# Units from 10 on become TensorE's moving rows against regrouped halves of older units, with 33 rounds added before their sum

## The reference

```python
e = jnp.stack([tbl_0[ids[:, 0]], ..., tbl_39[ids[:, 39]]], axis=1)   # 512 x 40 x 64
i_idx, j_idx = np.triu_indices(40, k=1)
viW = jnp.einsum('bpd,pde->bpe', e[:, i_idx, :], L0_rec_W)           # 780 matrices of 64 x 64
z = jnp.einsum('bpe,bpe->bp', viW, e[:, j_idx, :])
h = jnp.concatenate([z, dense_ctx], axis=1)                          # 512 x 796
h = jnp.maximum(h @ W_top1 + b_top1, 0.0)                            # 512 wide
h = jnp.maximum(h @ W_top2 + b_top2, 0.0)                            # 256 wide
y = h @ W_top3
```

## Time and profile before

| | us |
|---|---|
| median of 3 runs | 315.83 (315.57 to 318.13) |
| profiled execution, its own time | 316.28 |
| span of its trace, first to last instruction | 314.0 |
| PE busy | 307.4 (98%) |
| DVE busy | 255.2 (81%) |
| POOL busy | 193.2 (62%) |
| ACT busy | 135.6 (43%) |

### The profile page before, as it was taken

How to read it: one execution, slowest core, us unless ns; L and a number is a source line. 1 busy time by engine, 2 the same in 40 slices (tenths; PEclk the granted TensorE clock), 3 DMA queues, 4 the chain that set the end, 5 groups by cost and what they waited for, 6 DMA issues and landing times.

```text
span 314.0 us, 4400 instructions
## 1 busy us (share of the span) xinstructions
PE 307.4 (98%) x1676; PEld 112.0 (36%) x1676; DVE 255.2 (81%) x262; ACT 135.6 (43%) x338; POOL 193.2 (62%) x156
## 2 busy tenths in 40 slices
PE   7999999999999999999999999999999999999996
PEld 2444233333333323333333333333333333333464
DVE  4992999889898888989989999999999999950000
ACT  0497874875539545659974602066000000001032
POOL 3887777777777777777733887746665555650000
PEclk9999999999999999999999999999999999999999
DMA  5936232323223743232325689886779664440000
GB/s 147 316 113 206 66 92 62 93 61 79 74 62 94 277 149 91 58 92 64 92 54 118 142 192 179 166 191 153 167 167 188 139 135 92 94 83 8 10 0 0
DMA packets 16188, 35.87 MB, mean 114 GB/s; under 512 B 3748, under 2 KB 4776, under 8 KB 14504
## 3 DMA queue, kind: packets, MB, share of 16 engines
q0 software_dynamic: 5824, 16.79, 27.6%
q1 hardware_dynamic: 8264, 14.20, 15.1%
q10 hardware_dynamic: 2080, 4.61, 4.2%
HBM read 22.87 MB, written 0.00 MB: 73 GB/s over the span
## 4 chain that ended last, share of the span: by engine, by line
PE 63%; POOL 24%; issue 8%; DMA 3%; DVE 0%; ACT 0%; ACTq 0%
PE y_ps L671 39%; POOL gathered L338 24%; PE z_ps L695 14%; PE y_ps L705 5%; PE t_ps L705 2%; DMA gathered<-in_tbl,ids_sb 2%; PE y_ps L759 2%; DMA ids_sb<-ids_rows 1%; PE t_ps L759 1%; DVE prod L559 0%; PE y_ps L768 0%; ACT prod L472 0%; ACTq L368 0%; ACT y_out L475 0%; DVE x_fold L527 0%
## 5 line engine op out<-in xcount | busy, mean ns | idle before, releaser
L671 PE MATMUL y_ps<-x,w 64*128 64x512 f32 x780 | 182.8, 604 | 0.9 <-DVE prod L559 0.8
L338 POOL DMA_INDIRECT gathered<-in_tbl,ids_sb x128 | 127.6, 997 | 43.4 <-issue 38.4
L559 DVE TENSOR_TENSOR prod<-y_ps,x 128x1024 f32<-128x1024 f32 x89 | 103.8, 1210 | 15.3 <-PE y_ps L671 14.4
L559 DVE TENSOR_TENSOR prod<-y_ps,x_quad 128x1024 f32<-128x1024 f32 x96 | 110.4, 1214 | 1.3 <-issue 0.6
L671 PEld LDWEIGHTS y_ps<-x,w 64*128 64x128 f32 x780 | 70.2, 186 | 113.4 <-issue 81.3
L410 ACT COPY x<-x_fold 32x128 f32<-32x128 f32 x240 | 70.9, 295 | 68.4 <-DVE x_fold L527 65.7
L363 POOL TENSOR_TENSOR prod<-prod 128x2048 f32<-128x2048 f32 x12 | 54.5, 4540 | 33.2 <-DVE prod L559 33.2
L695 PE MATMUL z_ps<-prod,select 128*32 128x512 f32 x588 | 73.4, 600 | 0.0
L439 ACT COPY zT<-z_ps 128x512 f32<-128x512 f32 x6 | 3.5, 586 | 69.7 <-PE z_ps L695 69.7
L695 PEld LDWEIGHTS z_ps<-prod,select 128*32 128x32 f32 x588 | 14.3, 108 | 52.0 <-issue 36.8
L433 ACT COPY x_mix<-x 64x512 f32<-64x512 f32 x40 | 24.7, 617 | 0.7
(11 more groups left out here) (46 smaller groups left out, 89.1 us busy)
## 6 DMA issues: line engine op xcount, KB each, us to landing
w<-w_rows SPq DMA_DIRECT2D x48, 256.0 KB, 2.8
prod<-prod POOLq DMA_DIRECT2D x12, 1024.0 KB, 7.7
gathered<-in_tbl,ids_sb POOLq DMA_INDIRECT x128, 2.5
w<-w_rows ACTq DMA_DIRECT2D x1, 1792.0 KB, 8.2
prod<-in_tbl ACTq DMA_DIRECT2D x6, 256.0 KB, 7.8
prod<-hot_ids SPq DMA_DIRECT2D x4, 256.0 KB, 6.7
prod<-in_tbl ACTq DMA_DIRECT2D x4, 128.0 KB, 3.0
w<-w_rows ACTq DMA_DIRECT2D x1, 512.0 KB, 9.8
```

Of the source, the lines that this page charges most:

```text
L338: nc.gpsimd.indirect_dma_start(gathered[:, slot, c, s * DIM:(s + 1) * DIM], None, tables[f][:, :], bass.IndirectOffsetOnAxis(ap=ids_sb[:, ...
L559: nc.vector.tensor_tensor(prod[:, d % PROD_SLOTS, :, :], y_ps[:, d % DUO_SLOTS, :, :], factor, ALU.mult).then_inc(prod_ready, 1)
L671: last = nc.tensor.matmul(y_ps[:, d % DUO_SLOTS, half, :], w[rows, r % W_SLOTS, d % ROUND, :], x[rows, units[half], :], start=True, stop=True)
```

## The change

- The pair rounds end with unit 9 (`PAIRED = 10`) instead of 13. From unit 10 on a new unit u supplies the moving rows of PE's matmuls, and the columns are the regrouped halves of all older units c, two units each (`quads_of`). So every unit from 0 to 17 needs its `x_quad` copies: 72 instead of 24, each at the place that `QUAD_AT` names.
- Quad rounds begin at round 11. Of the 37 rounds from 11 to 47, 33 are added: 18 by 1 MB DMAs (12 before) and 15 by POOL (12 before). Round 12 and the rounds 14, 16 and 30 are summed in full. The lag of three begins at round 12 instead of 25; rounds 12 and 13 have no sum, and only round 13 has a block of the first layer in its place.
- 65 gathers are issued first (120 before). The other 63 come in batches of 7, 3 or 4 behind the DMA adds of rounds 11 to 39.
- `x` has 12 slots, `gathered` 4 (6 before), `w` 6 (8 before). Unit u and unit u + 12 share a slot.
- Unit 11 is transposed by PE (before round 12's third duo) instead of folded. `w1` is loaded in seven DMAs behind rounds 3 to 9 instead of one behind round 12. Two one-hots go from ACT to DVE, and two duos are put ahead of the last part of unit 3's pick.

```diff
-LAYER1_AT = [25, 26]
-GATHER_SLOTS = 6
-W_SLOTS = 8
-
-PAIRED = 14
-QUADS = (UNITS - PAIRED) // 2
+NO_SUMS_AT = [12, 13]
+GATHER_SLOTS = 4
+X_SLOTS = 12
+DUOS_AHEAD = 2
+W1_LOADED_AT = 3
+W_SLOTS = 6
+
+PAIRED = 10
+QUADS = UNITS // 2 - 1
...
-           14: (66, 70), 15: (74, 78), 16: (82, 86), 17: (90, 94), 18: (100, 104), 19: (116, 132)}
...
+FOLD_AT = {5: (4, 7), 6: (8, 12), 7: (16, 19), 8: (22, 26), 9: (29, 33), 10: (36, 40), 12: (53, 57), 13: (63, 68),
+           14: (72, 77), 15: (86, 100), 16: (109, 118), 17: (127, 133), 18: (141, 151), 19: (161, 169)}
...
-GATHERED_FIRST = 120
-GATHERS_BEHIND = {24: 2, 26: 2, 28: 2, 30: 2}
...
+GATHERED_FIRST = 65
+GATHERS_BEHIND = {11: 7, 13: 7, 15: 7, 17: 3, 19: 3, 21: 3, 23: 3, 25: 3, 27: 3, 29: 7, 31: 3, 33: 3, 35: 3, 37: 4, 39: 4}
+ADDED_BY_DMA = [11, 13, 15, 17, 19, 21, 23, 25, 27, 29, 31, 33, 35, 37, 39, 41, 43, 45]
+ADDED_BY_POOL = [18, 20, 22, 24, 26, 28, 32, 34, 36, 38, 40, 42, 44, 46, 47]
...
+        self.rounds = [pairs[i:i + ROUND] for i in range(0, len(pairs), ROUND)]
+        self.quads_of([10, 11])
+        self.rounds.append(later + self.mixed(11)[1:])
+        self.quads_of([12, 13])
+        self.quads_of([14, 15])
+        self.rounds.append(self.mixed(11)[:1] + self.mixed(15))
+        self.quads_of([16, 17])
+        self.quads_of([18, 19])
+        self.rounds.append(self.mixed(19))
...
+    def quads_of(self, units):
+
+        items = [(u, c) for u in units for c in range(u // 2)]
+        for (u, c), (v, e) in zip(items[::2], items[1::2]):
+            self.rounds.append([("low", u, c), ("low", v, e), ("high", u, c), ("high", v, e)])
...
             def save_half(u, s):
+                if s == 0 and u >= X_SLOTS:
+
+                    act.wait_ge(prod_ready, plan.last_row(u - X_SLOTS) + 1)
                 act.wait_ge(unit_folded, 2 * list(FOLD_AT).index(u) + s + 1)
...
+            def copy_quad(u):
+                act.wait_ge(x_ready, u + 1)
+                for s in range(2):
+                    for h in range(2):
+                        n = 2 * (u % 2) + s
+                        last = nc.scalar.copy(x_quad[n * QUAD:(n + 1) * QUAD, u - u % 2 + h, :],
+                                              x[s * DIM + h * QUAD:s * DIM + (h + 1) * QUAD, u % X_SLOTS, :])
+                last.then_inc(quad_ready, 1)
...
-                if r == 12:
-                    act.dma_start(w1[:, :, :], w1_in).then_inc(w1_loaded, 16)
...
+                if W1_LOADED_AT <= r < W1_LOADED_AT + NBLK:
+                    b = r - W1_LOADED_AT
+                    act.dma_start(w1[:, b, :], w1_in[:, b, :]).then_inc(w1_loaded, 16)
...
-                if r in LAYER1_AT:
-
-                    n = LAYER1_AT.index(r)
-                    pe.wait_ge(w1_loaded, 32)
-                    pe.wait_ge(z_saved, n + 1)
-                    layer1(0, full[n:n + 1], first=n == 0)
+                if r == NO_SUMS_AT[-1]:
+
+                    pe.wait_ge(w1_loaded, 16 * (NBLK + 1))
+                    pe.wait_ge(z_saved, 1)
+                    pe.wait_ge(x_ready, max(PE_TRANSPOSES_AT) + 1)
+                    layer1(0, full[:1], first=True)
```

More of the change, by code:

```diff
@@ L80, in __init__ @@
         for u in range(PAIRED):
-            pairs += [("pair", k, u) for k in range(u - u % 2)]
+            own = [("pair", k, u) for k in range(u - u % 2)]
+            later = own[-2:] if u == PAIRED - 1 else []
+            pairs += own[:len(own) - len(later)]
             if u % 4 == 3:
                 pairs += self.mixed(u)
[L84 to L99, removed]
+        self.rounds = [pairs[i:i + ROUND] for i in range(0, len(pairs), ROUND)]
[7 more added lines that the diff above has]
+        self.rounds.append(self.mixed(19))
         assert all(len(r) == ROUND for r in self.rounds[:-1])
@@ L109, in __init__ @@
         assert all(self.is_quad(r) for r in ADDED_BY_DMA + ADDED_BY_POOL)
+        assert list(QUAD_AT) == list(range(2 * QUADS))
+    def quads_of(self, units):
+        items = [(u, c) for u in units for c in range(u // 2)]
+        for (u, c), (v, e) in zip(items[::2], items[1::2]):
+            self.rounds.append([("low", u, c), ("low", v, e), ("high", u, c), ("high", v, e)])
     def mixed(self, u):
@@ L118, in sums_at, with last_row @@
     def sums_at(self, r):
-        if r < LAYER1_AT[0]:
+        if r < NO_SUMS_AT[0]:
             return r - EARLY_LAG if r >= EARLY_LAG else None
-        return None if r in LAYER1_AT else r - LAG
+        return None if r in NO_SUMS_AT else r - LAG
     def is_quad(self, r):
         return self.rounds[r][0][0] == "low"
-    def first_round(self, u):
-        if u >= PAIRED:
-            return self.quad_start[(u - PAIRED) // 2]
-        return next(d for d, duo in enumerate(self.duos) if u in duo[1:]) // ROUND
+    def last_row(self, u):
+        return max(d for d, (kind, k, c) in enumerate(self.duos)
+                   if u == k or kind == "pair" and u == c or kind.startswith("mix") and k <= u < k + 4)
     def transposed_at(self, u):
@@ L139, in transposed_at @@
             return FOLD_AT[u][0]
-        return next(d for d, duo in enumerate(self.duos) if u in duo[1:])
+        return PE_TRANSPOSES_AT[u]
     def tile_pairs(self, d, half):
@@ L413, in save_half, with mix_columns, begin_mixture @@
                     last.then_inc(x_ready, 1)
-                if s == 1 and u >= PAIRED:
-                    act.wait_ge(x_ready, u + 1)
-                    for s in range(2):
-                        for h in range(2):
-                            n = 2 * (u % 2) + s
-                            last = nc.scalar.copy(x_quad[n * QUAD:(n + 1) * QUAD, u - PAIRED - u % 2 + h, :],
-                                                  x[s * DIM + h * QUAD:s * DIM + (h + 1) * QUAD, u, :])
-                    last.then_inc(quad_ready, 1)
-            def save_mixture(k):
+            def copy_quad(u):
[6 more added lines that the diff above has]
+                last.then_inc(quad_ready, 1)
+            def mix_columns(k, units):
+                for n, kind in enumerate(("mix1", "mix2")):
+                    for half, (_, columns) in enumerate(plan.mixture(kind, k)):
+                        for side, (unit, field) in enumerate(columns):
+                            if unit in units:
+                                copied = nc.scalar.copy(x_mix[side * DIM:(side + 1) * DIM, 2 * n + half, :],
+                                                        x[field * DIM:(field + 1) * DIM, unit % X_SLOTS, :])
+                return copied
+            def begin_mixture(k):
                 if k:
@@ L625, in pick_unit @@
                 if u == HOT_UNITS - 1:
+                    for d in range(DUOS_AHEAD):
+                        interact(d)
                     transpose_unit(HOT_UNITS)
@@ L671, in interact @@
                     last = nc.tensor.matmul(y_ps[:, d % DUO_SLOTS, half, :], w[rows, r % W_SLOTS, d % ROUND, :],
-                                            x[rows, units[half], :], start=True, stop=True)
+                                            x[rows, units[half] % X_SLOTS, :], start=True, stop=True)
                 last.then_inc(y_ready, 1)
```

72 lines of the change are left out of this document (43 added, 29 removed).

## The result

| | before | after |
|---|---|---|
| median, us | 315.70 (4 runs, 315.51 to 318.13) | 353.64 (4 runs, 352.52 to 354.75) |
| profiled execution, us | 316.28 | 352.52 |
| span of its trace, us | 314.0 | 350.3 |
| PE busy, us | 307.4 (98%) | 317.1 (91%) |

The ratio is 1.1153, with a 95% interval of 1.1093 to 1.1214. The forecast was 350.7, in a range from 324 to 365.

What follows compares the result with a forecast made beforehand. PE bounds the kernel, and DVE as much in added rounds. The 37 rounds take 218.6 us instead of 185.9, +32.7; with 1.3 for block 0 and 0.9 at the end, +34.9: 350.7, range 324 to 365.

Steps and rivals of the forecast that it cites:

- As much the bound as PE: In added rounds DVE's products take 4.57 us and PE 4.62, so DVE bounds there as much as PE.
- The row on which all rests: Gathers queued behind a 1 MB add wait: first 8.2 us after its start, second 9.0, third 9.8, fourth 10.6.
- The rival that went by it: Gathers do not wait for the DMA add ahead of them: 310.3 us; chance 0.10.
- waits of 40.4: DVE's waits for gathers behind DMA adds, at the folds of units 12 to 19: 40.4 us, 20 with lower bounds.
- at full clock: The forecast's own case: waits behind adds while PE's clock stays full, 350.7 us; chance 0.78.
- 40.4 + 0.9 + 2.3: Rounds 11 to 47: gather waits 40.4 us, DVE's loss in round 12 0.9, the wait for block 4's save 2.3.
- The rival that the clock falls: PE's clock halves at its pauses, 4.7 us for each of 12, giving 407 us; chance 0.05.
- `z_saved`: PE waits for block saves standing behind copies in ACT's queue: 1.3 us for block 0, 2.3 for block 4.
- as gone: The wait for the late gather at 111.36, put down to the single 1.75 MB `w1` load: 1.9 us removed.
- The end: One block of the first layer moves from a round to the end: 0.9 us more.
- What would show it: Signs: some 12 DVE gather waits, 40 us in all; PE's share about 86%; 516 sum instructions, some 64 us.
- Half-clock slices: A sign that the forecast is wrong, which would put the time far above the range.

Runs made afterwards that it cites:

- the run with both causes removed: Changed kernel with the half-folds of units 12 to 19 up to 4 duos later and `MIX_AT` of unit 16 at 180 instead of 169: 316.76 us, ratio 1.0006.
- the run with zeros: Changed kernel with 4 to 18 matmuls of zeros for PE at nine folds, fitted to the length of each pause: 353.87 us, ratio 1.1172.
- The first run with zeros: Changed kernel with eight matmuls of zeros for PE at each of ten folds: 353.86 us, ratio 1.1186.
- the half adds: Changed kernel with DMA adds of 0.5 MB, only the first duo's half, PE summing three duos in these rounds: 330.31 us, ratio 1.0421.

## Why the prediction was right, and where its sum was not

**What bounds.** "As much the bound as PE" holds, and what holds DVE held the end: the time went with DVE's waits for gathers. DVE alone is not the bound, though. In the run with both causes removed PE was busy 179.0 of 183.9 us and DVE 174.8, so neither has much room, and PE the less.

**The row on which all rests.** It holds, in batches of three to seven too. From the add's start to a fold that waited, by POOL's and DVE's timelines of the changed kernel:

| gather behind the add | forecast | measured |
|---|---|---|
| first | 8.2 | 8.3, 8.2, 10.2 |
| second | 9.0 | 9.0 |
| third | 9.8 | 9.3, 10.2, 9.3, 10.6 |
| fourth | 10.6 | 9.6, 9.6 |

So 0.8 for each further gather was too much: the earliest thirds and both fourths came 0.3 after the one before. Three gathers were late by 0.4 to 2.0, and the runs do not show why. That these misses cancel over the ten halves (+0.1) is luck. The rule of the Trainium skill in DMA: Bandwidth & Descriptors, section "Two DMAs through the same engine are not ordered", by which a later descriptor may be complete ahead of an earlier one's writes, is not contradicted; here it gains nothing, since no gather's packet moved in the 6.9 us of the add shown above. The rival that went by it, 310.3, is out.

**The term "waits of 40.4".** In the changed kernel it measured 29.7. The step that failed is "at full clock": I gave the falls 0.05, as a world in which PE would run at the lower level for whole rounds, 407. They came with seven of its pauses, for 27.3 us in all, and took the place of waits. The two halves without a wait (6.8 of the forecast) each follow a half-clock stretch, in which DVE had already lost 2.0 and 2.7 to PE. With fewer falls the same term measures 37.9, near the forecast. The interval of 219.9 holds 44.9 beside DVE's 175.0, where the forecast had 40.4 + 0.9 + 2.3 = 43.6; the 12.0 of waits for PE, which include what came of the 2.3, and the two of 0.9 behind full sums fill what the gather waits leave. The total came out near the forecast because both kinds of wait are paid out of the same intervals, each from an add's start to its gathers' landing; the forecast had not seen this, and so far its agreement is luck.

**The rival that the clock falls.** The mechanism is there, its price was wrong. I had set 4.7 on top of each pause, a whole round at the lower level; measured, the time is the same with three stretches as with seven, and the one fall that no gather wait followed, in round 44 of the run with zeros, cost 1.4. TensorE: Matmul & The Clock Gate of the Trainium skill, section "HAM oscillation — how this bites in real kernels", tells of a clock that falls at every wait for a DMA. The trace agrees that it falls there, though with seven of the nine pauses of over 1 us that PE made behind DVE from round 11 on, and differs on the loss, as the next gather wait absorbs it.

**`z_saved`.** Block 4 cost 2.4 for a forecast 2.3. Block 0 cost nothing: PE has no such wait there. Rounds 0 to 10 did take 1.4 more, near the forecast 1.3, but from another cause, so that this term came out is luck. DVE's timeline of the changed kernel has two gather waits there:

```profile
70.56 0.45 DVE L562 STREAM_TRANSPOSE x_fold<-gathered 128x256 f32<-128x256 f32 x1 [1.09 <-DMA gathered<-in_tbl,ids_sb]
...
81.07 0.45 DVE L562 STREAM_TRANSPOSE x_fold<-gathered 128x256 f32<-128x256 f32 x1 [1.84 <-DMA gathered<-in_tbl,ids_sb]
```

I had counted the wait of `w1` "as gone", and these two stand in its place, though not surely by it. Two things came late. POOL issues its gathers back to back, 1.25 us apart, and the last gather for the fold at 81.07 was issued at 77.03 (74.87 in the kernel before); and it landed 4.0 after its issue, for the 2.5 of the earlier trace rows:

```profile
77.03 0.95 POOL L348 DMA_INDIRECT gathered<-in_tbl,ids_sb  x1 [0.30 <-issue]
```

The first run with zeros has the same loads of `w1`, issued this gather at 75.1 and has no gather wait ahead of round 11. So when POOL's gathers begin, which differs between executions, has a part in it; what share the loads have is not shown.

**The end.** The block moved there cost 0.9 (39.0 from round 47 to the end, for 38.1), as forecast.

**What would show it.** Twelve waits (ten of them behind adds, where I had listed 13), PE behind DVE behind gathers, and 516 sums came as said. PE's share was 91%, not 86%, and the sums took 68.2 us, not 64; with the clock full, in the run with both causes removed, PE's busy time is 301.4, as forecast. Half-clock slices, named as a sign of a time far above the range, were there without it.

## What to carry to other kernels

In this queue, small transfers issued behind a 1 MB add moved only when its packets were through, although the engine that issued them seemed idle. So before moving small transfers behind a large one, put their consumer at least the large one's landing later. Waits and slow clock that fall into the same interval do not add; price the interval once, from its start to the arrival, and price the slow clock only where no such wait follows. And before counting an engine's saved work as time, look at what it will wait for in the new order: here PE had 6.4 us less to do in 37 rounds, DVE left room for it, and 2.0 came through, because PE then stood 4.9 us, mostly for copies and saves on ACT.

## What was not expected of the hardware

- With pauses of 2.2 to 4.1 us PE's granted clock was 0.50 for 27.3 us in seven stretches, and full again each time while PE worked without a pause. The pauses of 1.6 and 1.9 us, which end at 221.21 and 246.48, were followed by none, but neither was the 2.38 that ends at 290.61, nor one of 2.45 that ends at 168.39 in the run with both causes removed. The same 2.38 ahead of round 44's sum was followed by a fall in the run with fitted zeros. So the length of a pause alone does not decide it; what does, stays open.
- The accumulating DMA's landing falls with its size, though not in proportion: 8.0 us for 1 MB, 4.7 for 0.5 MB.
- Twelve of a sum's matmuls take as long as sixteen, 1.92 us, and eight take 1.06. In the trace of the half adds the twelve start in groups of four, four, two and two, 0.43 apart, and the sixteen in four groups of four.
